# Softplus series in PSUM, a reordered scan tail, and a low-rank expert stage computed with expert rows on partitions

## The reference

```python
x = x + tanh(g_xattn[0]) * ssm(ctx, z=layernorm(x))       # block 1
x = x + tanh(g_ffn[0]) * low_rank_experts(layernorm(x))   # block 2
x = x + tanh(g_xattn[1]) * attention_16(layernorm(x), ctx)# block 3, and so on

# ssm: 256 channels, 16 states
delta = softplus(w_dt @ dt_lo + dt_b)
state = state * exp(delta * A) + (delta * u) * B_t        # a scan over 256 tokens
y = (sum_n state * C + D * u) * silu(z)

# low_rank_experts: 8 experts of rank 64
probs = softmax(x @ Wr.T + br)
h = einsum('nd,erd->ner', x, A);  y = einsum('ner,eor->neo', h, B) / 64
out = y[argmax(probs)] * max(probs)
```

## Time and profile before

| what | us |
| --- | --- |
| median of three runs | 1026.83 (1024.70 to 1027.12) |
| the profiled execution | 1026.77 |
| its span in the trace | 1025.0 |
| ssm stage: up to the first scan | 43.66 |
| ssm stage: scans | 43.66 to 128.97 |
| ssm stage: tail | 128.97 to 143.6 |
| low-rank stage | 143.6 to 190.4 |
| rest | 190.4 to 1025.0 |

### The profile page before, as it was taken

One profiled execution on the slowest core, in us unless ns is written; L12 is line 12 of the kernel. 1 busy time (PEld: TensorE's weight loads), 2 busy tenths in 40 slices (PEclk: granted clock), 3 DMA queues, 4 the chain that ended last, 5 costly groups with the idle time before them and its releaser, 6 DMA issues. The chain is left out here.

```text
span 1025.0 us, 17396 instructions
## 1 busy us (share of the span) xinstructions
PE 889.4 (87%) x5612; PEld 554.8 (54%) x5612; DVE 707.8 (69%) x1405; ACT 609.5 (59%) x1196; POOL 403.5 (39%) x339
## 2 busy tenths in 40 slices
PE   9599948999999999997697688998649999957697
PEld 4455535624777777775376553332425666644445
DVE  6989957889766676666788658995452334248875
ACT  5589944687777777776564366888303433205472
POOL 2798610376545454542231280000023676310132
PEclk9899979999999999999899799999869999979989
DMA  2332029000000000000000201400393333240001
GB/s 84 106 124 99 6 107 345 12 1 16 17 20 15 21 17 21 15 15 4 3 1 1 58 2 54 134 2 2 118 354 88 64 72 47 32 118 0 1 1 42
DMA packets 44239, 57.29 MB, mean 56 GB/s; under 512 B 5656, under 2 KB 35104, under 8 KB 44176
## 3 DMA queue, kind: packets, MB, share of 16 engines
q1 hardware_dynamic: 37680, 48.33, 14.0%
q0 software_dynamic: 4416, 6.03, 3.5%
q10 hardware_dynamic: 2080, 2.10, 0.6%
HBM read 49.90 MB, written 6.49 MB: 55 GB/s over the span
## 5 line engine op out<-in xcount | busy, mean ns | idle before, releaser
L1413 POOL TENSOR_TENSOR a_scratch<-a_scratch,a_inverse 128x512 f32<-128x512 f32 x64 | 66.5, 1039 | 115.2 <-DVE a_inverse L1549 115.2
L2626 PE MATMUL bank<-wup,moe_xT 128*128 x184 | 83.0, 594 | 1.3 <-ACT moe_xT L2688 1.2
L2410 DVE TENSOR_REDUCE a_tops<-bank 128x4 f32<-128x1024 f32 x64 | 77.7, 1223 | 8.5 <-PE bank L2090 5.5
L2861 DVE TENSOR_TENSOR moe_act_f<-bank,moe_silu 128x512 f32<-128x512 f32 x23 | 15.9, 692 | 92.4 <-ACT moe_silu L2695 80.6
L2258 ACT ACTIVATE wup<-bank,a_exp_scale 128x1024 f32<-128x1024 f32 x64 | 71.2, 1114 | 13.7 <-PE bank L2113 13.7
L567 POOL TENSOR_TENSOR ssm_drive<-ssm_du,ssm_b_row 128x1024 f32<-128x1024 f32 x32 | 75.6, 2392 | 8.4 <-DVE ssm_state L638 4.6
L638 DVE TENSOR_TENSOR_SCAN ssm_state<-bank,ssm_drive 128x512 f32<-128x512 f32 x64 | 74.8, 1209 | 1.1 <-issue 0.4
L1332 ACT ACTIVATE a_scratch<-bank,a_bias,a_q_factor 128x256 f32<-128x256 f32 x128 | 71.1, 560 | 7.1 <-DVE a_bias L1536 6.8
L1144 PE MATMUL bank<-keys,a_scratch 128*128 (+1 forms) x256 | 68.6, 390 | 2.0 <-DVE xn L1476 0.7
L2688 ACT COPY moe_xT<-bank 128x256 f32<-128x256 f32 x23 | 8.6, 373 | 99.5 <-PE bank L2614 99.5
L412 PE MATMUL bank<-ssm_seen,ident 128*128 128x512 f32 x124 | 65.8, 614 | 1.1 <-ACT ssm_seen L502 1.1
(11 more groups left out here) (504 smaller groups left out, 2336.0 us busy)
## 6 DMA issues: line engine op xcount, KB each, us to landing
ssm_b_row<-ssm_b_spill SPq DMA_DIRECT2D x16, 512.0 KB, 3.6
wup<-in_l_up_dram SPq DMA_DIRECT2D x8, 1024.0 KB, 10.0
a_wq_in<-in_l1x_q_dram SPq DMA_DIRECT2D x32, 128.0 KB, 2.1
wdn<-in_l_down_dram SPq DMA_DIRECT2D x8, 512.0 KB, 11.1
keys<-in_l1x_o_dram SPq DMA_DIRECT2D x1, 2048.0 KB, 12.1
X<-in_x_dram SPq DMA_DIRECT2D x1, 1024.0 KB
lora_raw<-in_l_gate_dram SPq DMA_DIRECT2D x1, 1024.0 KB, 7.0
lora_raw<-in_l_up_dram SPq DMA_DIRECT2D x1, 1024.0 KB, 9.0
```

The lines of the kernel that those rows point to most:

```text
L1413: pool.tensor_tensor(prob[:, j, :, :], prob[:, j, :, :], inverse[:, j, :].unsqueeze(2).to_broadcast([P, 2, SEQ]), ALU.mult).then_inc(S["p_ ...
L2410: dve.tensor_reduce(tops[:, f // 2 % 3, :, first:first + 2].rearrange("p q h -> p h q"), bank[:, at:at + 2, :].rearrange("p h (q n) -> p h ...
L2626: last = pe.matmul(bank[:, 2 * (i % 2) + m, :], xT[:, i % 2, c, :], wup[:, bass.ds(e, 1), c * 2 * FF + m * FF:c * 2 * FF + (m + 1) * FF] . ...
```

## The change

1. **Series.** The series of both halves is computed in banks 4 and 5 in place of SBUF; `small` stays in SBUF. Half 1 waits until half 0 has been copied out. The `skip_term` products of pieces 0 and 1, which also go to banks 4 and 5, move on PE behind that.
2. **Tail.** PE turns all four pieces of the last state ahead of the gather of the state before. ACT loads the silu table, makes the gates and two silu tiles ahead of its last `weigh`. Behind the last gather PE runs 12 `keep_busy` matmuls once all four `close` are done; ahead of the loop there are 4 in place of 8.
3. **Loads.** The five weight tiles of the low-rank stage and a new one, `low_select`, are held outside the stages and loaded in the first microseconds of the ssm stage.
4. **Low-rank stage.** `hidden` now works on groups: 128 expert rows on partitions by 512 tokens, eight groups (`j`, `h`). Six of them stand on PE ahead of the turned routing choice `hot`. `hot` is turned to [8 x 1024], ACT copies it to bf16, and PE spreads it over the expert rows by a one-pass bf16 matmul with `low_select` (`spread`), ACT copies the mask to SBUF, and DVE multiplies group by mask (`choose`). The product already lies as `out` needs it, so the eight turns and their copies are gone. The expert's weight is applied in `add`. The DVE work for the later stage stands at other places in the list.

```diff
-        series, sums = conv, conv
+        sums = conv
@@ ssm, PE
-                skip_term(0)
-                skip_term(1)
...
+                pe.wait_ge(S["delta_ready"], CC)
+                skip_term(0)
+                skip_term(1)
                 await_emptied(pe, ("z", 2))
-                keep_busy(8, ring((0, 0)))
+                keep_busy(4, ring((0, 0)))
...
-                turn((LAST, 2))
-                turn((LAST, 3))
+                for r in range(ROUNDS):
+                    turn((LAST, r))
+                gather(LAST - 1, 3)
                 gather(LAST, 2)
                 gather(LAST, 3)
+                pe.wait_ge(S["y_ready"], ROUNDS)
+                keep_busy(12, 2)
@@ ssm, ACT
-                weigh(LAST, 2)
                 act.preload_act_table_set("silu_and_others")
...
                 for r in range(ROUNDS):
+                    if r == 2:
+                        weigh(LAST, 2)
@@ ssm, DVE
+                    series, e = bank[:, 4:6, :], two(small[:, k, :])
+                    chain(dve.tensor_scalar(series, e, LOG1P[0], None, ALU.mult))
                     for c in LOG1P[1:]:
-                        chain(dve.scalar_tensor_tensor(series[:, k, :], series[:, k, :], c, small[:, k, :], ALU.add, ALU.mult))
+                        chain(dve.scalar_tensor_tensor(series, series, c, e, ALU.add, ALU.mult))
@@ low rank, PE
-                def hidden(t):
+                def hidden(g):
+                    j, h = GROUPS[g]
+                    await_count(pe, masked, g - 5)
                     for c in range(DC):
+                        last = pe.matmul(bank[:, H_BANK[g], :], wA[:, c, j * P:(j + 1) * P], core.xnT[:, c, h * HALF:(h + 1) * HALF],
+                def spread(g):
+                    j, h = GROUPS[g]
+                    pe.wait_ge(chosen_ready, 2)
+                    await_count(pe, mask_ready, g - 1)
+                    pe.matmul(bank[:, M_BANK[g % 2], :], core.low_select[:, j * P:(j + 1) * P], chosen[:, h * HALF:(h + 1) * HALF],
+                              start=True, stop=True).then_inc(spread_done, 1)
                 def out(t):
+                    pe.wait_ge(masked, 4 * (t // 4) + 4)
                     if t >= 2:
                         pe.wait_ge(added, t - 1)
...
+                for g in range(1, 6):
+                    hidden(g)
+                pe.wait_ge(hot_ready, 1)
...
+                for g in range(4):
+                    spread(g)
+                hidden(6)
+                spread(4)
+                hidden(7)
+                for t in range(3):
+                    out(t)
+                    spread(5 + t)
+                out(3)
+                pe.wait_ge(sums, 3)
@@ low rank, DVE
+                def choose(g):
+                    j, h = GROUPS[g]
+                    dve.wait_ge(h_done, g + 1)
+                    dve.wait_ge(mask_ready, g + 1)
+                    dve.tensor_tensor(hmT[:, j, h * HALF:(h + 1) * HALF], bank[:, H_BANK[g], :], mask[:, g % 2, :], ALU.mult
+                                      ).then_inc(masked, 1)
```

209 lines of the change are left out of this document (108 added, 101 removed).

## The result

The changed kernel takes **1028.75 us** in the median of 16 runs (1026.78 to 1031.81), the kernel before, timed beside it, 1026.0 (1022.18 to 1029.82): a ratio of 1.003, interval 1.0018 to 1.0043. A second measurement gave 1028.68 and 1.0016 (0.9999 to 1.0033), which by itself would not tell it from no change. So it is slower, by 0.2 to 0.3%. The forecast of 1024.4 was wrong in its sign, and the time lies just beyond the range's upper end of 1028.5.

A forecast was written before the change was run, and what follows sets the result against it. DVE's instruction times were taken to bound the stretch up to the first scan, a chain of waits the low-rank stage. The terms -6.5 - 2.3 - 1.9 + 5.0 + 1.7 + 1.6 gave -2.4, so 1024.4 us; range 1020.0 to 1028.5.

The forecast's parts named there:

- Term 1: Up to the first scan: series steps in PSUM escape contention with POOL, 1.29 us each, -6.5 us.
- The rival that DVE into PSUM is no cheaper: Series: instructions reading and writing PSUM take the contended 3.26 us, giving +7.4 us, 1034.2; chance 0.07.
- Term 2: Scan loop's start: no PE pause, full clock, DVE's 2.3 us wait for a turned piece goes, -2.3 us.
- Term 3: State-space tail: DVE's wait for silu(z) goes as gates and table load come earlier, -1.9 us.
- Term 4: Low-rank stage up to DVE's first product: five hidden groups delay the turned choice, 4.1 us later.
- Term 5: Rest of low-rank stage: DVE waits for masks 5 and 7 and the mean, together 6.0 us, 0.9 more.
- the third rival: Low-rank chain longer: half clock ahead of out(2) or in the first hiddens, 1.6 to 3.4 us more; chance 0.15.
- Term 6: PE pauses ahead of out(3) and at the low-rank stage's end halve the clock: +1.7 and +1.6 us.
- The short stage: Low-rank stage: if PE bounds it, its list ends 7 us ahead of before, giving 1012; chance 0.03.

The follow-up runs named there:

- e2: Kernel before with the series in PSUM and the new tail with its twelve zero matmuls, old loads and old low-rank stage: 1016.97 us, ratio 0.99.
- e12: Kernel before, unchanged, measured and profiled once more: 1026.47 us, ratio 0.9996.
- e15: Changed kernel with the old low-rank stage put back and without the twelve zero matmuls in the tail: 1016.21 us, ratio 0.9902.
- e9: Changed kernel with PE's order alone changed, choice turned behind hidden(2) and the first four spreads between the next groups: 1025.56 us, ratio 0.9988.
- e5: Changed kernel with zero matmuls added at two PE pauses, eight ahead of out(3) and ten behind out(7): 1021.34 us, ratio 0.9955.
- e3: Changed kernel with the new low-rank stage alone undone, so series, tail and early loads stay: 1012.00 us, ratio 0.9856.
- e8: Changed kernel with the same low-rank instructions in another order on PE, DVE and ACT: 1009.11 us, ratio 0.9833.

## Why the prediction was wrong, point by point

- **Term 1, series in PSUM: right.** -6.8 for -6.5. The step of 1.29 is 1.25, the opening 1.2 is 1.22, the copy 1.3 is 1.33, `du` with its contention 1.50. The rule of the Trainium skill (SBUF — State Buffer, Who interferes with whom) on two SBUF inputs beside GpSimd holds once more: the same three steps beside POOL products take 9.85 us with two SBUF inputs and 3.76 with one. That a PSUM operand holds a float32 TENSOR_SCALAR at the plain rate (the Trainium skill, VectorE: DVE Perf Modes, Why PSUM operands drop a tier) agrees too: 0.69 us without one, 1.22 with one. The rival that DVE into PSUM is no cheaper is dead.
- **Term 2, start of the loop: right**, -3.0 for -2.3. The clock was up from 36 us on, 0.7 us more than the wait alone.
- **Term 3, tail: right**, -1.8 for -1.9; DVE goes from the weigh at 122.43 into `close` without a wait.
- **Term 4: right**, 19.4 us to the first product for 19.3.
- **Term 5 and the third rival: the step that failed.** The waits were the right three, but 10.3 us long in place of 6.0, or 7.7 with the slow `out(3)`. The 2.6 between stand at mask 4 (0.56 for nothing), mask 5 (3.27 for 1.8), mask 7 (2.56 for 2.35), the mean (3.77 for 3.5), and one of 0.18. Those at masks 4 and 5 come for the most part (by estimate 1.7 of 2.0 us, 3.60 less 1.9) from `hidden(6)` at half clock, 3.60 us in place of 1.9, which stands in PE's queue ahead of the spread of mask 4, of `out(0)` and so of mask 5. I had judged pauses one by one, from a single profile: 2.3 us harmless, 2.86 not. Here 1.14 and 0.55 us, with two short spreads between them, came ahead of the fall. And the 2.3 us were not harmless: the same pause of the old stage was followed by half clock in three of the seven profiles that have it (e2, e12, e15). e9 shows it from the other side. The rival that came nearest (1026 to 1027.8, chance 0.15) had the kind right and the place wrong: it looked to `out(2)` or the first `hidden`s, and `out(2)`, behind 1.91 us, took 1.97, at full clock.
- **Term 6: right in kind, small in size.** Both clocks fell. `out(3)` lost 1.8 (1.7 forecast), block 3's start 2.5 (1.6, with a bound of 2), since nearly all of the sixteen passes, 6.18 us, ran low and not some 3.2 us of them. e5 gives both back.
- **What the sum makes of it.** -11.7 in the state-space stage for -10.7; 3.7 beyond the forecast in the low-rank stage and at block 3, 2.6 of them from term 5 and 0.9 from term 6: +0.3 at the keys for -2.4. The profile behind the keys adds 0.6. The last 1.9 us of the median's +2.75 are in no profile and open. So terms 5 and 6 turn the forecast's gain into nothing, and what makes it a loss is for the greater part not explained. The range was too narrow by it, since I had put the whole uncertainty ahead of block 3.
- **A step that nobody took.** The prediction gave the early loads no price and asked only what the new stage does with them. e3 shows that they are worth 4 to 5 us with the old stage. The changed kernel lost them, like all else, in its order.
- **The short stage** had 0.03 for "if PE were what bounds it". e8 makes PE the bound, and there the stage is 17.5 us shorter than in the changed kernel. The layout was good for it, only the order was not.

## What to carry to other kernels

When work is moved ahead of a decision, look at what stands in the same queue *behind* it: five `hidden` groups ahead of the turned choice hid nothing and held up DVE, ACT and PE itself by turns. Put the short instruction that releases another engine as early as its input allows, and fill the waits so made with work that has no input (here the row sums); the same instructions were 19.6 us faster so. Measure each part of a large change alone: this one held a gain of 14.8 us and a loss of 16.7, and read as a whole it looked like nothing.
